# Tridiagonalization by Householder steps: sums with A u taken directly, norm work moved up, TensorE calls padded to 128 columns and constant calls put into its waits

## What is computed

```python
deg = jnp.sum(A, axis=0) + jnp.sum(A, axis=1) - jnp.diagonal(A)
d_inv_sqrt = jnp.where(deg > 0, jax.lax.rsqrt(deg), 0.0)
L_norm = d_inv_sqrt[:, None] * (jnp.diag(deg) - A) * d_inv_sqrt[None, :]
_, U = jnp.linalg.eigh(L_norm)
agg = jnp.einsum('mn,bnd->bmd', U.T, features)
```

## Time and profile before

| | us |
|---|---|
| median of 3 runs (range) | 3256.26 (3255.88 to 3257.19) |
| the profiled execution, its own time | 3255.26 |
| its span, first to last instruction | 3253.6 |
| of it from the first to the last step's new x (L366) | 27.8 to 1464.6 |
| busy TensorE / VectorE / ScalarE / GpSimd | 1931.9 / 2272.8 / 794.6 / 255.3 |

### The profile page before, as it was taken

The page is one execution under the profiler, slowest core; times in us unless marked ns, Lnnn a source line. Parts: engine busy times, 40 slices in busy tenths (PEclk is TensorE's granted clock), DMA queues, the critical chain, the costliest instruction groups (busy, mean ns, idle before and its releaser), DMA issues. The chain is left out here.

```text
span 3253.6 us, 40850 instructions
## 1 busy us (share of the span) xinstructions
PE 1931.9 (59%) x8496; PEld 1684.1 (52%) x8496; DVE 2272.8 (70%) x13811; ACT 794.6 (24%) x2948; POOL 255.3 (8%) x367
## 2 busy tenths in 40 slices
PE   6777877778555555551000004057697788788777
PEld 6777777777444444441000003046476676677666
DVE  6666766667888787778999999967544544554553
ACT  1111111111111111112000001025344344344434
POOL 0000000000000000003222223001100000000000
PEclk9999999999999999997555556578898888888888
DMA  0000000000000000001000000002000000000000
GB/s 23 1 1 1 1 1 1 1 1 0 1 1 1 1 1 1 1 1 43 0 1 0 1 1 1 1 20 64 26 7 6 13 13 0 13 13 0 13 6 7
DMA packets 23030, 22.99 MB, mean 7 GB/s; under 512 B 1584, under 2 KB 19664, under 8 KB 22736
## 3 DMA queue, kind: packets, MB, share of 16 engines
q1 hardware_dynamic: 20304, 13.15, 1.4%
q0 software_dynamic: 2560, 8.39, 0.8%
HBM read 13.15 MB, written 8.39 MB: 7 GB/s over the span
## 5 line engine op out<-in xcount | busy, mean ns | idle before, releaser
L297 PE MATMUL bank<-R,A 128*128 128x2 f32 x1280 | 308.7, 352 | 0.0
L297 PEld LDWEIGHTS bank<-R,A 128*128 128x128 f32 x1280 | 303.7, 333 | 0.0
L303 PE MATMUL bank<-Qp,const 128*128 128x4 f32 x768 | 205.2, 361 | 164.8 <-DVE Qp L404 164.8
L303 PEld LDWEIGHTS bank<-Qp,const 128*128 128x128 f32 x768 | 182.8, 318 | 186.9 <-DVE Qp L404 186.9
L667 DVE SCALAR_TENSOR_TENSOR q<-rec,nb,q 128x14 f32<-128x14 f32 (+1 forms) x1270 | 277.2, 257 | 0.0
L331 ACT ACTIVATE nrm<-nx,tiny 128x1 f32<-128x1 f32 x256 | 75.4, 294 | 756.7 <-DVE nx L381 756.7
L663 DVE RECIPROCAL rec<-q 128x14 f32<-128x14 f32 (+1 forms) x1270 | 247.9, 237 | 11.8 <-DVE q L667 1.4
L1399 ACT ACTIVATE gate<-bank,gbias 128x128 f32<-128x128 f32 (+3 forms) x576 | 208.8, 432 | 174.9 <-PE bank L1354 137.2
L286 PE MATMUL bank<-R 128*128 128x10 f32 (+15 forms) x768 | 204.1, 374 | 61.7 <-DVE R L366 58.9
L286 PEld LDWEIGHTS bank<-R 128*128 128x128 f32 x768 | 183.0, 319 | 86.8 <-issue 83.9
L774 PE MATMUL bank<-tq,const 128*128 128x1 f32 x2 | 0.6, 361 | 367.1 <-DVEq L854 367.1
(11 more groups left out here) (363 smaller groups left out, 4612.3 us busy)
## 6 DMA issues: line engine op xcount, KB each, us to landing
xnext<-in_x SPq DMA_DIRECT2D x16, 256.0 KB, 3.4
x_scratch<-x1out POOLq DMA_DIRECT2D x16, 256.0 KB, 3.6
xin<-x_scratch SPq DMA_DIRECT2D x16, 256.0 KB, 2.8
out<-yout POOLq DMA_DIRECT2D x16, 256.0 KB, 2.7
const<-in_consts SPq DMA_DIRECT2D x1, 1495.5 KB, 6.3
adjN<-in_adj SPq DMA_DIRECT2D x1, 256.0 KB, 6.5
wqkv<-in_L_gnn_Wqkv SPq DMA_DIRECT2D x1, 192.0 KB, 7.8
W<-in_L_gnn_W SPq DMA_DIRECT2D x2, 64.0 KB, 3.5
```

Source lines behind the costliest of these rows:

```text
L297: last = mm(pZ[:, u, :], A[:, t, u * P:(u + 1) * P], R[:, t, 0:XE], start=(t == tiles[0]), stop=(t == tiles[-1]))
L303: last = mm(pG[:, :], ones, Qp[:, t, :, :].rearrange("p a b -> p (a b)"), start=(t == tiles[0]), stop=(t == tiles[-1]))
```

## The change

- TensorE calls of 1 to 34 columns become calls of 128 columns. `R` gets 126 zero columns ahead of x and e, `xx` and `Qp` become 128 columns wide with zeros in the unused ones; A times (x, e), the `dots`, the sums of squares and the sums over rows all move 128 columns. The heads stay as they are.
- Constant calls `keep_warm` (all-ones matrix times the identity, into an unused bank, nobody reads them) are put in after A times (x, e) and after the sums over rows: 2 and 2 a step in the two-tile stage, 3 and 4 in the one-tile stage.
- The products x x and x e are formed together right after the new x and ahead of `Pe`, so that one TensorE call sums both (n2 and x0), and the copy of x0 goes. In the one-tile stage this call stands ahead of the `dots`.
- `tau` (the former sigma with the other sign), u, `hh`, beta are formed before A times (x, e) is used; `Au` = Ax + tau Ae is multiplied with x and u, and TensorE sums x Au and u Au directly: one call instead of two (two-tile) or one (one-tile), and `rc`, `crd`, `xmA`, `xm`, `xAu`, `v1`, `uAu` go, `uA`, `om`, `bR` (and `gsum` in the two-tile stage) come in.
- ScalarE takes over n2/2, and the next unit vector waits for A times (x, e).

The diff, cut to its core:

```diff
-        XE = 2
-        R = sb("R", [P, T2, XE + 2 * PANEL])
+        LEAD = 126
+        XC, EC, PC = LEAD, LEAD + 1, LEAD + 2
+        R = sb("R", [P, T2, PC + 2 * PANEL])
+        SQ = max(2 * T2, LEAD + 2)
+        xx = sb("xx", [P, SQ])
+        Qp = sb("Qp", [P, SQ])
...
+                def keep_warm(calls):
+                    for _ in range(calls):
+                        mm(banks[7][:, 0, 0:P], ones, ident1, start=True, stop=True)
...
+                            lead = w if LEAD else PC
+                            at = PC + w - lead
+                            def x_dots():
+                                pe.wait_ge(h_x, k + 1)
+                                if j:
+                                    for t in tiles:
+                                        last = mm(dots[:, 0, 0:at], R[:, t, XC:EC].broadcast_to([P, P]), R[:, t, lead:PC + w],
+                                                  start=(t == tiles[0]), stop=(t == tiles[-1]))
+                                    last.then_inc(h_D, 1)
+                            def squares():
+                                pe.wait_ge(h_xx, k + 1)
+                                mm(pS[:, own], ones, xx[:, own], start=True, stop=True).then_inc(h_s, 1)
...
-                            for t in tiles:
-                                last = mm(dots[:, 0, 0:XE + w], R[:, t, 0:1].broadcast_to([P, P]), R[:, t, 0:XE + w],
-                                          start=(t == tiles[0]), stop=(t == tiles[-1]))
-                            last.then_inc(h_D, 1)
-                            pe.wait_ge(h_xx, k + 1)
-                            mm(pN2[:, 0:len(tiles)], ones, xx[:, tiles[0]:T2], start=True, stop=True).then_inc(h_s, 1)
+                            if lone:
+                                squares()
+                                x_dots()
+                            else:
+                                x_dots()
+                                squares()
...
-                                    last = mm(pZ[:, u, :], A[:, t, u * P:(u + 1) * P], R[:, t, 0:XE],
+                                    last = mm(pZ[:, u, 0:PC], A[:, t, u * P:(u + 1) * P], R[:, t, 0:PC],
                                               start=(t == tiles[0]), stop=(t == tiles[-1]))
                             last.then_inc(h_z, 1)
+                            keep_warm(3 if lone else 2)
                             pe.wait_ge(h_q, k + 1)
-                            for t in tiles:
-                                last = mm(pG[:, :], ones, Qp[:, t, :, :].rearrange("p a b -> p (a b)"),
-                                          start=(t == tiles[0]), stop=(t == tiles[-1]))
-                            last.then_inc(h_g, 1)
+                            mm(pG[:, own], ones, Qp[:, own], start=True, stop=True).then_inc(h_g, 1)
+                            keep_warm(4 if lone else 2)
...
                             A_(nrm[:, :], n2, ACT.Sqrt, bias=tiny[:, :]).then_inc(h_nrm, 1)
+                            A_(half_n2[:, :], n2, ACT.Copy, scale=0.5).then_inc(h_half, 1)
+                            def next_unit():
+                                act.wait_ge(h_z, k + 1)
+                                A_(R[:, here, EC:PC], unit[:, here, bass.ds(k + 2, 1)], ACT.Copy).then_inc(h_e, 1)
...
+                            def correction():
+                                dve.wait_ge(h_pe, k)
+                                dve.wait_ge(h_w, k)
+                                dve.wait_ge(h_D, blk * (PANEL - 1) + (first // PANEL * (PANEL - 1) + j))
+                                return ch.mark(v.tensor_tensor(Ec[:, here, :, 0:w], ...
+                            if j and not lone:
+                                i_E = correction()
                             dve.wait_ge(h_s, k + 1)
-                            v.tensor_reduce(n2, pN2[:, 0:nt], AX.X, ALU.add).then_inc(h_n2, 1)
+                            v.tensor_reduce(nx[:, :], pS[:, own].rearrange(by_sum, c=2), AX.X, ALU.add).then_inc(h_n2, 1)
+                            if j and lone:
+                                i_E = correction()
...
                             i_nrms = ch.mark(v.tensor_tensor(nrms[:, :], nrm[:, :], sgn[:, :], ALU.mult))
+                            ch.reach(i_nrms)
+                            i_tau = ch.mark(scaled(tau, n2s[:, :], inv[:, :], nrms[:, :]))
+                            if lone:
+                                i_zr = Ax()
+                            ch.reach(i_tau)
+                            scaled(u, e, tau, x).then_inc(h_u, 1)
+                            i_hh1 = ch.mark(v.scalar_tensor_tensor(hh1[:, :], tau, 0.5, x0, ALU.mult, ALU.add))
+                            i_om = ch.mark(v.tensor_tensor(om[:, :], tau, x0, ALU.add))
+                            if lone:
+                                ch.reach(i_zr)
+                                i_Au = ch.mark(scaled(Au[:, here], r, tau, z))
+                            i_rtau = ch.mark(v.reciprocal(rtau[:, :], tau))
...
+                            i_hh = ch.mark(scaled(hh[:, :], hh1[:, :], tau, half_n2[:, :]))
+                            if not lone:
+                                v.reciprocal(beta, hh[:, :]).then_inc(h_b, 1)
+                                i_bR = ch.mark(v.tensor_tensor(bR[:, :], beta, rtau[:, :], ALU.mult))
+                                i_uA = ch.mark(v.scalar_tensor_tensor(uA[:, here], u, bR[:, :], below_h, ALU.mult, ALU.mult))
+                                i_zr = Ax()
+                                i_Au = ch.mark(scaled(Au[:, here], r, tau, z))
+                            v.tensor_tensor(q_by_tile, R[:, here, XC:PC + w + 2:PC + w + 1 - XC],
+                                            Au[:, here].unsqueeze(2).broadcast_to([P, nt, 2]), ALU.mult).then_inc(h_q, 1)
...
+                            v.tensor_scalar(p, Au[:, here], beta, None, ALU.mult).then_inc(h_p, 1)
+                            ch.link(scaled(zz[:, here], p, om[:, :], r, ALU.subtract))
                             i_zzm = ch.mark(v.tensor_tensor(zzm[:, here], zz[:, here], below_h, ALU.mult))
                             dve.wait_ge(h_g, k + 1)
+                            if lone:
+                                xa, ua = pG[:, 2:3], pG[:, 3:4]
+                            else:
+                                xa, ua = gsum[:, 0:1], gsum[:, 1:2]
+                                ch.link(v.tensor_reduce(gsum[:, :], pG[:, own].rearrange(by_sum, c=2), AX.X, ALU.add))
+                            scaled(x, uA[:, here], xa, zzm[:, here], ALU.subtract).then_inc(h_x, 1)
+                            i_k2 = ch.mark(v.tensor_scalar(k2[:, :], ua, beta, nbeta[:, :], ALU.mult, ALU.mult))
+                            v.tensor_tensor(by_tile, R[:, here, XC:EC].broadcast_to([P, nt, 2]), R[:, here, XC:PC], ALU.mult).then_inc(h_xx, 1)
                             scaled(Pe[:, here, w + 1], u, k2[:, :], p).then_inc(h_w, 1)
```

More of the change, by code:

```diff
@@ L242, in build @@
         stat = sb("stat", [P, 2])
-        sigma, beta = stat[:, 0:1], stat[:, 1:2]
+        tau, beta = stat[:, 0:1], stat[:, 1:2]
         nx = sb("nx", [P, 2])
-        xx = sb("xx", [P, T2])
+        n2, x0 = nx[:, 0:1], nx[:, 1:2]
+        gsum = sb("gsum", [P, 2])
         kept = sb("kept", [P, N, 2])
@@ L248, in build @@
         flip = sb("flip", [P, N])
-        half_n2, nrm, sgn, n2s, nrms, inv, hh1, hh, rsig, crd, xAu, v1, uAu, k2, nbeta = (sb(n, [P, 1]) for n in
-            ("half_n2", "nrm", "sgn", "n2s", "nrms", "inv", "hh1", "hh", "rsig", "crd", "xAu", "v1", "uAu", "k2", "nbeta"))
+        nrm, half_n2, sgn, n2s, nrms, inv, om, hh1, hh, rtau, bR, k2, nbeta = (sb(n, [P, 1]) for n in
+            ("nrm", "half_n2", "sgn", "n2s", "nrms", "inv", "om", "hh1", "hh", "rtau", "bR", "k2", "nbeta"))
         PHASES = ((0, (0, 1)), (P, (1,)))
@@ L253, in build @@
         with nc.Block() as block:
[L254 to L263, removed]
+            h_x, h_xx, h_e, h_s, h_D, h_n2, h_z, h_nrm, h_half, h_q, h_g, h_u, h_pe, h_p, h_b, h_nb, h_w, h_T, h_Tc, h_dl, h_A, h_step, h_end = (
+                sem(n) for n in ("x_ready", "squares_ready", "unit_ready", "squares_summed", "dots_ready", "norm2_ready", "Ax_ready", "norm_ready", "half_ready",
+                "products_ready", "sums_ready", "u_ready", "u_kept", "p_ready", "beta_ready", "stat_kept", "w_ready", "panel_turned",
+                "panel_copied", "update_ready", "A_updated", "step_dve", "end_dve"))
+            dots = banks[0][:, :, :]
+            pZ = banks[1]
+            pG = banks[2][:, 0, :]
+            pS = banks[6][:, 0, :]
             pPe, pPd, pDelta = banks[3], banks[4], banks[5]
@@ L347, in _ @@
                 v = nc.vector
-                v.memset(tiny[:, :], 1e-35).then_inc(h_end, 1)
-                v.tensor_tensor(R[:, :, 0:1], A[:, :, 0:1], later[:, :, 0:1], ALU.mult).then_inc(h_x, 1)
-                dve.wait_ge(h_end, 1)
+                x_all = R[:, :, XC:EC]
+                v.memset(tiny[:, :], 1e-24)
+                if LEAD:
```

(38 more changed lines are left out.)

107 lines of the change are left out of this document (47 added, 60 removed).

## The result

| | before | after | predicted |
|---|---|---|---|
| median (range), us | 3256.55 | 3085.88 (3078.16 to 3087.03) | 3034 (2985 to 3120) |
| ratio, 95% interval | | 0.9471 (0.9454 to 0.9487) | 0.932 |
| span of the profiled execution | 3253.6 | 3085.4 | |
| 120 two-tile steps within panels, x to x | 693.2 | 618.5 | 580 |
| 120 one-tile steps within panels | 573.7 | 508.7 | 492 |

The lower rows are sums of the distances between starts of the new x in the trace. For the prediction they are 120 x 4.74 and 120 x 4.01, each with half of the 22 us for slow steps behind panel ends. The kernel is faster, inside the range; of the 221 us forecast some 170 came. Nearly all of it lies in the reduction, 167 us in the trace: what follows the last x took 1789.0 us before and 1787.8 after.

A forecast was written before the change was run, and what follows sets the result against it. Bound: a chain from x to x, TensorE then VectorE in two-tile steps, mostly VectorE in one-tile steps. Terms -120, -91, -33, +22 and +1 make -221 us against 3255.3, so 3034 us, range 2985 to 3120.

The forecast's parts named there:

- The clock: Reduction steps: run at 1.2 GHz before, 2.4 GHz after, with further passes spaced 0.11 us in place of 0.21.
- Two-tile step: Reduction, x to x at 2.4 GHz: 5.74 us becomes 4.74, a gain of 1.00 a step, -120 us for 120.
- The tail: End of the two-tile step: products with Au end at 3.75 us, the new x at 4.74.
- One-tile step: Reduction, x to x: 4.77 us becomes 4.01, a gain of 0.76 a step, -91 us for 120.
- The second rival: Reduction: the clock alternates; half of the 240 steps at 1.2 GHz, +1.42 or +1.55 us each, gives 3190 us; chance 0.08.
- Panel ends: Seven two-tile ends save 2.65 us each, seven one-tile ends 2.0, 1.4 with the clock down: -33 us (-20 to -38).
- the 0.90 for L318: Panel end: the update at L318, 2.07 us before, falls to 0.56 of its time, saving 0.90 us.
- A slow step behind each panel end: Start of each new panel: about one step at 1.2 GHz, partly hidden, +22 us for 16 (0 to +45).
- The first rival: Reduction: clock stays at 1.2 GHz, constant calls delay the dots; steps of 6.16 and 5.56 us, 3380 us total; chance 0.10.
- The third: VectorE's chain in each step: five waits cost 0.10 us each in place of 0.03, +84 us, 3118 total; chance 0.06.

The follow-up runs named there:

- no_pad: The changed kernel with its TensorE calls as narrow as before (no zero columns), constant calls kept; 3308.76 us, ratio 1.0156.
- more_calls: The changed kernel with six constant calls instead of two behind A times (x, e) in the two-tile steps; 3059.18 us, ratio 0.9402.
- best: The changed kernel with six constant calls for two in two-tile steps, more in panels' first steps (6 two-tile, 15 one-tile), and two hand-overs removed; 3012.66 us, 0.9252.
- old_sums_padded: The kernel before, own sums kept, small calls padded to 128 columns, constant calls added (1 and 2 a two-tile step, 2 and 4 a one-tile step); 3138.56 us, 0.9644.

## Why the prediction was right, and what it missed

- **The clock** went as forecast: padded calls and constant calls together brought 2.4 GHz, and the step's spacing of 0.11 a pass with it. The reading of the bare 1.00 of the earlier trace rows as 1.2 GHz is borne out by `no_pad`: under the same bare 1.00 its passes are spaced as in the earlier trace rows, and where its clock is recorded, a narrow pair takes 0.57 us at 0.50 and 0.36 at 1.00.
- **Two-tile step, 4.74 forecast, 4.95 measured**: 0.21 x 120 = 25 us. The terms that failed are hand-overs of "Two-tile step". "The `dots` (four passes, 0.05 + 0.68)": two waits stand ahead of them, 0.14, which cost the step 0.06. "`bR` ... at 3.0; `uA` starts there": it starts at 3.20 from x's end (219.13 - 215.93), 0.10 of it the address behind a wait. With both out the step is 4.78. The 0.04 that are left stand ahead of `nx`: without the second wait it starts 1.03 behind x's end, not 0.99, as the `dots` start 0.06 behind x and take 0.71. The tail is right: products to x 1.00, forecast 0.99.
- **One-tile step, 4.01 forecast, 4.12 as median of all**: 13 us, by the same two terms; without them 3.96, a little under the forecast. Two steps of each panel, the ninth and the fifteenth, take some 4.4 and 4.5 us at a recorded 1.00, 5 us in all; no run here shows why, and nothing in the sum stood for them.
- **The clock inside panels.** Nothing in the sum stood for the 27 two-tile steps with a stretch at 1.2 GHz, 17 us. The second rival named the place, TensorE's idle stretch ahead of the products with `Au`, but priced half the steps at +1.42; they were 27 of 112 at some +0.6, as a part of the step only ran slow. `more_calls` shows the cause by filling that stretch.
- **Panel ends, -33 forecast, -25 measured.** The one-tile ones saved 13.7 us, by the 2.0 each of the forecast. The two-tile ones saved 11.7 in place of 2.65 x 7 = 18.6: the 0.90 for L318 failed, as in seven of the eight panels this update still took 1.83 to 2.07 us. The forecast's bounds had this case, the clock down there. With six calls the seven save 18.8 (89.6 - 70.8).
- **A slow step behind each panel end**: +22 forecast, 17 measured (7 and 10), the right cause by `more_calls` and `best`.
- **The first rival** (clock stays) did not happen, but its two-tile step is `no_pad`'s. The forecast also put 3380 on a stage already at 2.4 GHz; that sum is worked out at 1.2 GHz, so it is no price of that case. **The third** (longer chain) was wrong in four of its five waits: u, `bR`, `Au` and x start 0.04 behind the end of what they need, as the root does in the earlier trace rows, where the forecast read 0.03; only `uA` has 0.14.

What the forecast lacks adds up: 38 us in the two-tile steps (25 + 17 less 4 in the first steps), 17 in the one-tile steps, 8 at the panel ends; 6 come back because the steps of before were longer on the whole than the two of the earlier trace rows, and 2 at the change of stage: 55, and 221 - 55 = 166 beside the trace's 167.

## What to carry to other kernels

Before counting on a clock, look at how passes are spaced, and price padding and filler calls together: here either alone cost time, and both together paid. Fill idle stretches of the engine up to its next real call, the ones at a loop's turn too, but not beyond it, and measure each fill: the four calls more in every two-tile step gave 27 us, those in the panels' first steps nothing that the time can tell. Look for a fall of the clock in windows of single steps, since a stage's mean of 0.9 hides it. In a chain of small operations, look at what stands behind a wait: an operand at a computed address cost 0.10 us a step, a second wait 0.06, together 46 us here, more than that fill.

## What the runs showed that was not expected

A TensorE busy for 94% of a stretch (784.66 of 833 us in `no_pad`) kept the spacing of 1.2 GHz all through it. The Trainium skill (TensorE: Matmul & The Clock Gate, Part 1) says that the gate follows how busy the engine has been. Taken as busy time in the profile, that would have brought this kernel to 2.4 GHz before the others, and the rows contradict it; what agrees with it is that filling idle stretches raised the clock, as in `best` (3.03 us idle made 0.75, a granted 0.70 made 1.00). `old_sums_padded`, busy 522.64 of 673 us, had a granted 0.94 in its two-tile stage:

```profile
27.00:700.00 673.00, 522.64 (x3368) 437.90 (x3368) 534.19 (x4081) 126.64 (x774) 0.00 (x0) 0.94 0.00 1
```

The zeros, which the first rival held against the change, did not keep the clock down: it rose though 126 of the 128 columns that A meets are zeros. What the clock does with other values there was not run.
